# Sixteen normalised activation tiles are transposed by DMA instead of by TensorE and ScalarE, in a two-layer kernel on eight cores

## The chip, the cores and the metric

One Trainium2 chip, all 8 of its cores. Each core runs the same program on its own 2,048 of the 16,384 tokens; the weights are the same for all of them and each core loads all of them. The metric is the device time of the slowest core, in microseconds (us); smaller is better.

## The reference

```
x = x + layernorm(einsum('bsk,nk->bsn', layernorm(x), weight1 * elem_mask))
x = x + layernorm(einsum('bsi,oi->bso', layernorm(x), sign(weight2)) + bias)
# x: (2, 8192, 4096); weight1, weight2: (4096, 4096); elem_mask: 32 x 32 blocks of 0 or 1
```

Two layers, each a layer norm, a 4096 x 4096 matrix product, a second layer norm and a residual. The first product has a block mask on its weights, the second has the signs of its weights.

## The kernel before

A core's tokens are 16 tiles of 128. The output of a layer is made in 8 slabs of 512 columns, and a slab's weights are 8 blocks of 512 rows of the reduction. A **unit** is 8 tiles by one slab: 8 blocks x 8 tiles x 4 matmuls of 128x512, that is 256 matmuls, with the 8 PSUM banks holding the 8 tiles' sums. The units run in this order: 0 to 7 are slabs 0 to 3 of layer 1, for tiles 0 to 7 and 8 to 15 in turn; 8 to 11 are slabs 4 to 7 for tiles 0 to 7; 12 to 15 are slabs 4 to 7 for tiles 8 to 15; 16 to 23 are the eight slabs of layer 2 for tiles 0 to 7; 24 to 29 are six of them for tiles 8 to 15, and the last two slabs of those tiles are the tail.

So layer 1 is complete for tiles 0 to 7 when unit 12 begins, and for tiles 8 to 15 when unit 16 begins. The step between the layers is spread over the units: VectorE's `residual(tt)` scales the first product's row by its statistics, adds the loaded x and takes the statistics of the sum, for two tiles in each of units 12 to 15 and for one tile in each of units 16 to 23. GpSimd's queue loads the rows and stores the sum in DRAM (`store_x1`), ScalarE normalises it in place (`normalise`, L861), and after the unit's last matmul TensorE transposes it in 128x128 pieces (`transposes`, L464), eight to a PSUM bank, which ScalarE copies back into the tile's place in HT (`evict_transposed`, L837). Only the transposed form can be the stationary operand of layer 2.

ScalarE has two other jobs there. In layer 1 it evicts the sums of each unit (`evict1`, L847). In units 15 to 22 it turns the next unit's 16 weight **pieces** (128x1024 float32, 512 KB) into signs in fp8 (`sign_piece`, L853), in its program ahead of that unit's evictions. SyncE's queue loads the pieces (`load_w2`, L360) into **stages**, slots of 4 KB a partition: ST has stages 0 to 6, YS 7 and 8, RING 9 to 12. A piece's load waits until the work that had its stage last is done (`wait_stage_free`). The fixed table in `_homes` says which stage each piece gets: the first 16 pieces of layer 2, which are signed in unit 15, have stages 2, 3 and 4 in turn, and the others 5, 6, 2, 3 and 4. Before these loads, SyncE's queue holds the reloads of layer 1's last masked blocks (L417).

Every engine works through its own instructions in the order in which they are written, and semaphores order them between engines. `wait_acc_out` waits until a PSUM bank has been evicted. Signed blocks are kept in DRAM too, and the units from 24 on read them back (RING then has `NQ` slots of a signed block). ME holds layer 1's block mask, which nothing reads after its last weight piece.

Of the kernel before, what the change touches and what calls it, by code (L numbers as in the profile page):

```python
# [14 lines left out]
F32 = mybir.dt.float32  # L15
BF16 = mybir.dt.bfloat16
F8 = mybir.dt.float8e4
I32 = mybir.dt.int32
AF = mybir.ActivationFunctionType
AX = mybir.AxisListType  # L20

D = 4096
# [9 lines left out]


NRING = 10
NQ = 20
N2 = 96
U_A1 = 12
U_B1 = 16
# [28 lines left out]
for _u in range(2, 31):  # L67
    if _u in MASK_END:
        START[_u + 1] = (START[_u] + 2) % 8
    elif 16 <= _u < 24:  # L70
        START[_u + 1] = (START[_u] + 4) % 8
    else:
        START[_u + 1] = START[_u]

# [26 lines left out]

STAGES = 13
FEED_RING = (1, 4, 0, 2, 3, 5, 6)
HOME = {}
BEFORE = {}
# [2 lines left out]
def _homes():  # L110
    last, count = {}, {}

    def put(piece, at):
        sw = "p" if piece[0] == "x" else "s"
        count[sw, at] = count.get((sw, at), 0) + 1
        HOME[piece] = (at, count[sw, at])
        BEFORE[piece] = last.get(at)
        last[at] = piece

    for g in range(16):  # L120
        put(("m", g), ((0, 1, 5, 6), (9, 10, 11, 12))[g // 4 % 2][g % 4])
    for p in range(16):
        put(("w", p), (2, 3, 4, 7, 8)[p % 5])
    for g in range(16, 32):
        put(("m", g), (0, 1, 4)[(g - 16) % 3])
    last[2] = last[3] = ("xt", 13)
    last[5] = last[6] = ("xt", 14)
    k = 0
    for u in range(1, 11):
        for kind, n in FEED[u]:  # L130
            for piece in ([("m", n)] if kind == "m" else [("w", 2 * n), ("w", 2 * n + 1)]):
                put(piece, FEED_RING[k % 7])
                k += 1
    for g in range(32):
        put(("x", g), (0, 1, 5, 6)[g % 4])
    for g in range(32, 64):
        put(("x", g), g % 2)
    for p in range(16):
        put(("z", p), 2 + p % 3)
    for p in range(16, 128):  # L140
        put(("z", p), (5, 6, 2, 3, 4)[(p - 16) % 5])


_homes()
# [7 lines left out]

SEMS = (["cst", "msk_rd", "wgt", "sgn", "rdy_bt", "rdy_me", "msk_mm", "xaggr", "xstat", "xn0", "xn1",
         "tr", "tev", "mm", "blk", "ev1", "ev2", "bns", "self", "xp", "x1stat", "x1norm",
         "ystat", "yt", "fo", "pool"]
        + ["ldS%d" % i for i in range(STAGES)] + ["ldP%d" % i for i in range(STAGES)]
        + ["ldX%d" % i for i in range(16)] + ["ldR%d" % i for i in range(NRING)]
        + ["stC%d" % i for i in range(NRING)] + ["stY%d" % i for i in range(2)]
# [6 lines left out]
def build():  # L165
# [19 lines left out]
    with es:  # L185
# [28 lines left out]
        RING8 = RING[:, :].bitcast(F8)  # L214
        PBH = pb[:, :].bitcast(BF16)
        HTF = HT[:, :].bitcast(F32)
        YSF = YS[:, :].bitcast(F32)
        RINGF = RING[:, :].bitcast(F32)
        RINGI = RING[:, :].bitcast(I32)
# [20 lines left out]

        def stage(piece, ints=False):
            at = HOME[piece][0]
            if at >= 9:
                return RINGI[:, (at - 3) * 1024:(at - 2) * 1024]
            if at >= 7:
                return YSF[:, (at - 7) * 1024:(at - 6) * 1024]
            return (STI if ints else ST)[:, at * 1024:(at + 1) * 1024]
# [72 lines left out]
        def wait_stage_free(eng, piece):  # L320

            o = BEFORE[piece]
            if o is None:
                return
            kind, k = o
            if kind == "xt":
                eng.wait_ge(sem["xn1"], k + 1)
            elif kind == "m":
                eng.wait_ge(sem["msk_rd"], k + 1)
            elif kind == "w":  # L330
                eng.wait_ge(sem["wgt"], k + 1)
            elif kind == "x":
                eng.wait_ge(sem["xp"], k + 1)
            else:
                eng.wait_ge(sem["sgn"], k + 1)
# [112 lines left out]
        def _(t):  # L448
# [85 lines left out]
            for u in range(2, 30):  # L534
                lay, base, slab = unit(u)
                n0 = unit_block0(u)
                frees = u >= 8 or u % 2 == 1
                for b in range(8):
                    for p in range(8):
                        i = (START[u] + p) % 8  # L540
                        if b == 0:

                            if u == 2 and i >= 4:
                                if i == 7:
                                    t.wait_ge(sem["rdy_me"], 5)
                                else:
                                    t.wait_ge(sem["tev"], 64)
                            elif u == 2:
                                t.wait_ge(sem["ev1"], 8 + 4 + i + 1)
                            elif 13 <= u <= 16:  # L550
                                t.wait_ge(sem["tev"], 64 + 8 * (u - 13) + p + 1)
                            elif 17 <= u <= 24 and p >= 4:
                                t.wait_ge(sem["tev"], 96 + 4 * (u - 17) + p - 4 + 1)
                            else:
                                wait_acc_out(t, u - 1, i)
                            if u - 1 in MASK_END and p == 7:
                                t.wait_ge(sem["rdy_me"], masks)

                            if u == 16:
                                t.wait_ge(sem["tev"], 64 + 4 * i + 4)  # L560
                            if u == 24:
                                t.wait_ge(sem["tev"], 96 + 4 * i + 4)
                        if p == 0:
                            wait_block_ready(t, n0 + b)
                        ins = visit(i, base + i, n0 + b, b == 0, b == 7)
                        if b == 7:
                            ins.then_inc(sem["mm"], 1)
                        elif p == 7 and frees:
                            ins.then_inc(sem["blk"], 1)
                        if b == 7 and p == 3 and u in MASK_END:  # L570
                            s = MASK_END[u]
                            t.wait_ge(sem["msk_rd"], 16 * s + 16)
                            wait_acc_out(t, u, START[u])
                            mask_sums(START[u], s, range(4))
                if u in MASK_END:
                    masks += 1
                    t.wait_ge(sem["rdy_bt"], masks)
                    wait_acc_out(t, u, (START[u] + 1) % 8)
                    t.matmul(bank((START[u] + 1) % 8), SEL[:, :], BTD[:, :], start=True, stop=True
                             ).then_inc(sem["msk_mm"], 1)  # L580
                if 12 <= u < 16:
                    for q in range(8):
                        tt = 2 * (u - 12) + q // 4
                        if q % 4 == 0:
                            t.wait_ge(sem["x1norm"], tt + 1)
                        wait_acc_out(t, u, (START[u] + q) % 8)
                        transposes(tt, q % 4, (START[u] + q) % 8)
                if 16 <= u < 24:
                    t.wait_ge(sem["x1norm"], u - 8 + 1)
                    for q in range(4):  # L590
                        wait_acc_out(t, u, (START[u] + q) % 8)
                        transposes(u - 8, q, (START[u] + q) % 8)


            for i in range(8):
# [237 lines left out]
        def _(a):  # L833
# [21 lines left out]

            def normalise(tt):

                slot = HT[:, tt * D:(tt + 1) * D]
                a.wait_ge(sem["x1stat"], tt + 1)
                a.wait_ge(sem["stX%d" % (tt % 2)], 16 * (tt // 2 + 1))  # L860
                a.activation(slot, slot, AF.Identity, bias=NM[:, tt:tt + 1], scale=RS[:, tt:tt + 1]  # L861
                             ).then_inc(sem["x1norm"], 1)

            def scale_y(seq, h):

# [43 lines left out]

            for u in range(2, 30):  # L910
                lay, base, slab = unit(u)
                if 13 <= u <= 16:
                    for q in range(8):
                        evict_transposed(2 * (u - 13) + q // 4, q % 4, (START[u - 1] + q) % 8,
                                         64 + 8 * (u - 13) + q)
                if 17 <= u <= 24:
                    for q in range(4):
                        evict_transposed(u - 9, q, (START[u - 1] + q) % 8, 96 + 4 * (u - 17) + q)
                for b in range(8):
                    if 15 <= u < 23:  # L920
                        n = unit_block0(u + 1) + b
                        wait_ring_slot(a, n)
                        sign_piece(n, 0)
                        sign_piece(n, 1)
                    if 12 <= u < 16 and b in (3, 6):
                        normalise(2 * (u - 12) + (b == 6))
                    if 16 <= u < 24 and b == 6:
                        normalise(u - 8)
                for tt in FIN.get(u, ()):
                    scale_y(tt, 0)  # L930
                    scale_y(tt, 1)
# [214 lines left out]
```

## Time and profile before

| | |
|---|---|
| median of 3 runs (lowest to highest) | 1949.73 us (1949.58 to 1951.43) |
| time of the profiled execution, and its span | 1950.22 us, 1948.7 us |
| spans of the eight cores | 1937.1 to 1948.7 us |
| TensorE busy | 1859.5 us (95%) |
| matmuls of the two products | 8192, 1786.8 us busy |
| ScalarE busy | 484.5 us (25%) |
| VectorE busy | 967.1 us (50%) |
| DMA, mean over the span | 471.53 MB, 242 GB/s |

The profile is of the slowest core of one execution. Busy time is the time in which an engine has an instruction in work; the span runs from the first instruction to the last. The granted clock is a share of TensorE's full 2.4 GHz. DMA share is the mean busy share of the core's 16 DMA engines in a stretch. A row of the chain that ended last has a start in us, a length in us, and what was at work.

### The profile page before, as it was taken

How to read it: one execution, taken by the hardware profiler on the slowest of the kernel's cores; microseconds unless marked ns; L12 is line 12 of the kernel's file. 1: busy time of each engine (PE TensorE's matmuls, PEld its weight loads, DVE VectorE, ACT ScalarE, POOL GpSimd, SP SyncE). 2: the span in 40 equal slices, each digit the busy share in tenths (PEclk: the TensorE clock that was granted, in tenths of full speed). 3: DMA queues.
4: the chain of work that ended last, by engine and by line, in shares of the span. 5: the costliest groups of instructions: out<-in, count | busy, mean ns of one | idle time of the engine just before them, and what ended most of it. 6: DMA issues, size and time to landing. Idle time of an engine off the chain costs nothing.

```text
span 1948.7 us, 26135 instructions; the slowest of 8 cores (1937.1 to 1948.7 us)
## 1 busy us (share of the span) xinstructions
PE 1859.5 (95%) x9483; PEld 875.6 (45%) x9483; DVE 967.1 (50%) x1441; ACT 484.5 (25%) x449; POOL 230.6 (12%) x420
## 2 busy tenths in 40 slices
PE   2689999999999999999999999999999999999996
PEld 1245444444444444444445444444444444444442
DVE  5778477666564330665533534433552333342465
ACT  2266300000000000133445444434420011110032
POOL 2444100000011000110101000000001011000110
PEclk8899999999999999999999999999999999999998
DMA  9998689976698764787799988898863566562494
GB/s 295 330 311 295 182 284 323 302 220 237 228 313 261 248 200 141 236 257 229 234 274 285 294 275 288 278 314 279 266 213 114 194 227 207 187 200 71 141 284 164
DMA packets 121791, 471.53 MB, mean 242 GB/s; under 512 B 13600, under 2 KB 13616, under 8 KB 106304
## 3 DMA queue, kind: packets, MB, share of 16 engines
q1 hardware_dynamic: 85248, 289.44, 47.4%
q0 software_dynamic: 36416, 180.41, 26.9%
q8 instruction: 77, 1.26, 0.3%
q14 instruction: 50, 0.41, 0.1%
HBM read 354.46 MB, written 115.34 MB: 241 GB/s over the span
## 4 chain that ended last, share of the span: by engine, by line
PE 83%; DMA 9%; DVE 3%; SPq 2%; issue 1%; POOL 1%; ACT 1%; DVEq 0%; ACTq 0%; POOLq 0%
PE pb L474 81%; DMA ST<-w2s 2%; DMA RING<-x 2%; DMA ST<-w1s 2%; PE pb L464 2%; DMA HT<-x 1%; DVE BNX L670 1%; SPq L383 1%; SPq L349 1%; DVE RING L662 1%; DVE RR L638 1%; DMA ST<-mask 0%; DMA ST<-x 0%; PE pb L456 0%; POOL HT L974 0%
## 5 line engine op out<-in xcount | busy, mean ns | idle before, releaser
L474 PE MATMUL pb<-RING,HT 128*128 128x512 bf16 (+1 forms) x8192 | 1786.8, 380 | 21.7 <-DVE RING L662 18.0
L474 PEld LDWEIGHTS pb<-RING,HT 128*128 128x128 bf16 x8192 | 800.3, 98 | 985.9 <-issue 37.8
L760 DVE TENSOR_TENSOR YS<-pb,RR 128x512 bf16<-128x512 f32 x112 | 77.3, 691 | 335.0 <-PE pb L474 334.9
L686 DVE BATCH_NORM_STATS2 BNST<-YS 128x6 f32<-128x512 bf16 x240 | 150.2, 682 | 152.7 <-ACT YS L847 151.5
L847 ACT ACTIVATE YS<-pb 128x512 bf16<-128x512 f32 x128 | 74.7, 600 | 539.7 <-PE pb L474 539.4
L662 DVE TENSOR_TENSOR RING<-ST,ME 128x1024 bf16<-128x1024 f32 x122 | 145.0, 1222 | 102.8 <-PE pb L474 70.4
L853 ACT ACTIVATE RING<-ST 128x1024 fp8e4<-128x1024 f32 x128 | 132.1, 1067 | 179.4 <-DMA ST<-w2s 179.2
L876 ACT ACTIVATE ST<-HT,NM,RS 128x2048 f32<-128x2048 bf16 x32 | 65.7, 2088 | 382.1 <-DVE NM L630 378.7
L638 DVE TENSOR_REDUCE RR<-ST 128x32 f32<-128x1024 int32 x120 | 142.4, 1212 | 25.1 <-DMA ST<-mask 24.3
L837 ACT ACTIVATE HT<-pb 128x1024 bf16<-128x1024 bf16 x128 | 122.3, 1041 | 130.6 <-PE pb L464 130.5
L743 DVE TENSOR_TENSOR HT<-HT,ST 128x1024 bf16<-128x1024 bf16 x64 | 75.6, 1223 | 90.6 <-DMA ST<-x 87.5
L861 ACT ACTIVATE HT<-HT,NM,RS 128x4096 bf16<-128x4096 bf16 x16 | 60.8, 3798 | 150.5 <-DMA x1d<-HT 128.5
L770 DVE TENSOR_TENSOR ST<-ST,HT 128x2048 f32<-128x2048 f32 x32 | 72.3, 2290 | 41.7 <-ACT ST L876 41.6
L464 PE MATMUL pb<-IDN,HT 128*128 128x128 bf16 x1024 | 72.3, 231 | 20.6 <-POOL HT L974 7.1
L987 POOL DMA_DIRECT2D y1d<-YS x32 | 24.7, 771 | 502.0 <-ACT YS L847 502.0
L464 PEld LDWEIGHTS pb<-IDN,HT 128*128 128x128 bf16 x1024 | 66.7, 104 | 33.3 <-issue 25.3
L746 DVE BATCH_NORM_STATS2 BNX<-HT 128x6 f32<-128x512 bf16 x128 | 77.5, 681 | 1.7
L670 DVE BATCH_NORM_STATS2 BNX<-HT 128x6 f32<-128x512 f32 x96 | 58.5, 679 | 37.1 <-DMA HT<-x 23.1
L987 POOL DMA_DIRECT2D y2d<-YS x28 | 21.5, 769 | 434.7 <-DVE YS L760 431.9
L999 POOL DMA_DIRECT2D ST<-x x64 | 34.4, 538 | 156.0 <-DVE HT L743 153.9
L884 ACT ACTIVATE HT<-HT,NM,RS 128x2048 bf16<-128x2048 f32 x16 | 33.5, 2093 | 47.9 <-POOL NM L967 47.9
L1023 POOL DMA_DIRECT2D out<-ST x32 | 17.3, 540 | 185.3 <-DVE ST L770 185.3
(53 smaller groups left out, 335.1 us busy)
## 6 DMA issues: line engine op xcount, KB each, us to landing
ST<-w2s SPq DMA_DIRECT2D x128, 512.0 KB, 12.5
ST<-w1s SPq DMA_DIRECT2D x122, 512.0 KB, 10.5
ST<-mask SPq DMA_DIRECT2D x120, 512.0 KB, 9.7
ST<-x POOLq DMA_DIRECT2D x64, 512.0 KB, 11.1
out<-ST POOLq DMA_DIRECT2D x32, 1024.0 KB, 6.9
HT<-x SPq DMA_DIRECT2D x24, 1024.0 KB, 20.6
y1d<-YS POOLq DMA_DIRECT2D x32, 512.0 KB, 4.4
c1d<-RING POOLq DMA_DIRECT2D x32, 512.0 KB, 9.0
```

The source lines that it names most:

```text
L464: ins = t.transpose(PBH[:, b * 1024 + e * 128:b * 1024 + (e + 1) * 128], HT[:, c:c + 128], IDN[:, :])
L474: ins = t.matmul(bank(b), HT[:, c:c + 128], w[:, e * 512:(e + 1) * 512], start=(first and e == 0), stop=(last and e == 3))
L638: v.tensor_reduce(RR[:, (s % 2) * 512 + q * 32:(s % 2) * 512 + q * 32 + 32], stage(("m", g), True).rearrange("p (a b) -> p a b", b=32), AX ...
L662: v.tensor_tensor(dst, src, mk, op=OP.mult).then_inc(sem["wgt"], 1)
L670: ins = v.bn_stats(BNX[:, q * 6:q * 6 + 6], xhalf(k, q // 4)[:, (q % 4) * 512:(q % 4) * 512 + 512])
L686: v.bn_stats(BNST[:, c:c + 6], YS[:, i * 512:(i + 1) * 512]).then_inc(sem["bns"], 1)
L743: v.tensor_tensor(part, part, stage(piece), op=OP.add).then_inc(sem["xp"], 1)
L746: ins = v.bn_stats(BNX[:, q * 6:q * 6 + 6], slot[:, q * 512:(q + 1) * 512])
L760: v.tensor_tensor(YS[:, i * 512:(i + 1) * 512], bank(i), BIA[:, (slab % 2) * 512:(slab % 2) * 512 + 512], op=OP.add).then_inc(sem["ev2"], 1)
L837: a.activation(HT[:, c:c + 1024], PBH[:, b * 1024:(b + 1) * 1024], AF.Identity).then_inc(sem["tev"], 1)
L847: a.activation(YS[:, i * 512:(i + 1) * 512], bank(b), AF.Identity).then_inc(sem["ev1"], 1)
L853: a.activation(ring(n)[:, h * 1024:(h + 1) * 1024], stage(("z", p)), AF.Sign, saturate=False).then_inc(sem["sgn"], 1)
```

## The change

TensorE's transposes between the units 12 to 24 and ScalarE's copies of them back to HT are gone. `normalise(tt)` now writes its result to another room: to stages 2 and 3 of ST for tiles 0 to 7, and to the last two bf16 slots of RING for tiles 8 to 15. `transpose_back(tt)` then issues one transposing DMA of 128 x 4096 bf16 (1 MB) from ScalarE's queue, from the room into HT. The wait for the tile's store to DRAM has moved from `normalise` to it, and `normalise` waits until the DMA of the tile before has landed (`x1tr`), since the room is one. Unit 16 waits for the DMAs of tiles 0 to 7 and unit 24 for those of 8 to 15. The stages 2 and 3 aren't free in unit 15 any more: the first 16 pieces of layer 2 use stage 4 and a new stage 13, in ME, and the others six stages. RING has 16 slots for signed blocks in the place of 20.

```diff
-NQ = 20
+NQ = 16
@@ _homes
+    last[2] = last[3] = ("t", 7)
+    last[13] = ("w", 127)
...
     for p in range(16):
-        put(("z", p), 2 + p % 3)
+        put(("z", p), (4, 13)[p % 2])
     for p in range(16, 128):
-        put(("z", p), (5, 6, 2, 3, 4)[(p - 16) % 5])
+        put(("z", p), (5, 6, 2, 3, 4, 13)[(p - 16) % 6])
@@ wait_stage_free
-            if kind == "xt":
+            if kind == "t":
+                eng.wait_ge(sem["x1tr"], 16 * (k + 1))
+            elif kind == "xt":
@@ TensorE, block 0 of a unit
-                            elif 13 <= u <= 16:
-                                t.wait_ge(sem["tev"], 64 + 8 * (u - 13) + p + 1)
-                            elif 17 <= u <= 24 and p >= 4:
-                                t.wait_ge(sem["tev"], 96 + 4 * (u - 17) + p - 4 + 1)
                             else:
                                 wait_acc_out(t, u - 1, i)
...
-                            if u == 16:
-                                t.wait_ge(sem["tev"], 64 + 4 * i + 4)
-                            if u == 24:
-                                t.wait_ge(sem["tev"], 96 + 4 * i + 4)
+                            if u == 16 or u == 24:
+                                t.wait_ge(sem["x1tr"], 16 * (base + i + 1))
@@ TensorE, after a unit
-                if 12 <= u < 16:
-                    for q in range(8):
-                        tt = 2 * (u - 12) + q // 4
-                        if q % 4 == 0:
-                            t.wait_ge(sem["x1norm"], tt + 1)
-                        wait_acc_out(t, u, (START[u] + q) % 8)
-                        transposes(tt, q % 4, (START[u] + q) % 8)
-                if 16 <= u < 24:
-                    t.wait_ge(sem["x1norm"], u - 8 + 1)
-                    for q in range(4):
-                        wait_acc_out(t, u, (START[u] + q) % 8)
-                        transposes(u - 8, q, (START[u] + q) % 8)
@@ ScalarE
             def normalise(tt):
 
-                slot = HT[:, tt * D:(tt + 1) * D]
+                room = STB[:, 2 * 2048:4 * 2048] if tt < 8 else RING[:, 8 * 2048:10 * 2048]
                 a.wait_ge(sem["x1stat"], tt + 1)
+                if tt == 8:
+                    wait_block_free(a, 88)
+                    wait_block_free(a, 89)
+                if tt > 0:
+                    a.wait_ge(sem["x1tr"], 16 * tt)
+                a.activation(room, HT[:, tt * D:(tt + 1) * D], AF.Identity,
+                             bias=NM[:, tt:tt + 1], scale=RS[:, tt:tt + 1]).then_inc(sem["x1norm"], 1)
+
+            def transpose_back(tt):
+
+                room = STB[:, 2 * 2048:4 * 2048] if tt < 8 else RING[:, 8 * 2048:10 * 2048]
+                a.wait_ge(sem["x1norm"], tt + 1)
                 a.wait_ge(sem["stX%d" % (tt % 2)], 16 * (tt // 2 + 1))
-                a.activation(slot, slot, AF.Identity, bias=NM[:, tt:tt + 1], scale=RS[:, tt:tt + 1]
-                             ).then_inc(sem["x1norm"], 1)
+                a.dma_start_transpose(HT[:, tt * D:(tt + 1) * D].rearrange("p (k t) -> p k t", k=32),
+                                      room).then_inc(sem["x1tr"], 16)
@@ ScalarE, units 2 to 29
-                if 13 <= u <= 16:
-                    for q in range(8):
-                        evict_transposed(2 * (u - 13) + q // 4, q % 4, (START[u - 1] + q) % 8,
-                                         64 + 8 * (u - 13) + q)
-                if 17 <= u <= 24:
-                    for q in range(4):
-                        evict_transposed(u - 9, q, (START[u - 1] + q) % 8, 96 + 4 * (u - 17) + q)
                 for b in range(8):
...
                     if 12 <= u < 16 and b in (3, 6):
                         normalise(2 * (u - 12) + (b == 6))
-                    if 16 <= u < 24 and b == 6:
+                        transpose_back(2 * (u - 12) + (b == 6))
+                    if 16 <= u < 24 and b == 5:
                         normalise(u - 8)
+                    if 16 <= u < 24 and b == 7:
+                        transpose_back(u - 8)
```

`START`, the bank with which a unit begins, also stays the same from unit 16 to 24, where it moved on by 4 at each.

How the instructions stand. TensorE, from unit 7's last block to unit 13 before (L474 are the products' matmuls, L464 the transposes, L579 a product for the block mask):

```order
L474 MATMUL pb<-RING,HT 128x512 x16
L579 MATMUL pb<-BTD,SEL 128x512
L474 MATMUL pb<-RING,HT 128x512 x1280
L464 MATMUL pb<-IDN,HT 128x128 x64
L474 MATMUL pb<-RING,HT 128x512 x256
```

and now, from the same place to the end of the program:

```order
L480 MATMUL pb<-RING,HT 128x512 x16
L579 MATMUL pb<-BTD,SEL 128x512
L480 MATMUL pb<-RING,HT 128x512 x6144
L185 UNCONDITIONAL_BRANCH
```

The 512 transposes (4 times 64 and 8 times 32) have left TensorE, and the matmuls of units 8 to 29 and of the tail follow each other. ScalarE in unit 15 before, from the copies of unit 14's transposes to the middle of the unit (L853 signs a piece from the stage that it waits for, L861 normalises tile 6):

```order
L837 ACTIVATE HT<-pb 128x1024 [waits tr] x8
L853 ACTIVATE RING<-ST 128x1024 [waits blk,ldS2]
L853 ACTIVATE RING<-ST 128x1024 [waits ldS3]
L853 ACTIVATE RING<-ST 128x1024 [waits blk,ldS4]
L853 ACTIVATE RING<-ST 128x1024 [waits ldS2]
L853 ACTIVATE RING<-ST 128x1024 [waits mm,ldS3]
L853 ACTIVATE RING<-ST 128x1024 [waits ldS4]
L853 ACTIVATE RING<-ST 128x1024 [waits mm,ldS2]
L853 ACTIVATE RING<-ST 128x1024 [waits ldS3]
L861 ACTIVATE HT<-HT,NM,RS 128x4096 [waits x1stat,stX0]
```

and now, from unit 14's evictions to the middle of unit 15 (L841 signs a piece, L853 normalises tile 6, L861 issues its transposing DMA):

```order
L835 ACTIVATE YS<-pb 128x512 [waits mm,stY1,bns] x4
L841 ACTIVATE RING<-ST 128x1024 [waits blk,ldS4]
L841 ACTIVATE RING<-ME 128x1024 [waits ldS13]
L841 ACTIVATE RING<-ST 128x1024 [waits blk,ldS4]
L841 ACTIVATE RING<-ME 128x1024 [waits ldS13]
L841 ACTIVATE RING<-ST 128x1024 [waits mm,ldS4]
L841 ACTIVATE RING<-ME 128x1024 [waits ldS13]
L841 ACTIVATE RING<-ST 128x1024 [waits mm,ldS4]
L841 ACTIVATE RING<-ME 128x1024 [waits ldS13]
L853 ACTIVATE ST<-HT,NM,RS 128x4096 [waits x1stat,x1tr]
L861 DMA_TRANSPOSE HT<-ST 128x32x128 [waits x1norm,stX0]
```

The eight copies ahead of the signs have gone, the pieces now alternate between two stages where there were three, and the DMA stands right behind the normalising, ahead of the next pieces. ScalarE in unit 12 now:

```order
L853 ACTIVATE ST<-HT,NM,RS 128x4096 [waits x1stat]
L861 DMA_TRANSPOSE HT<-ST 128x32x128 [waits x1norm,stX0]
L853 ACTIVATE ST<-HT,NM,RS 128x4096 [waits x1stat,x1tr]
L861 DMA_TRANSPOSE HT<-ST 128x32x128 [waits x1norm,stX1]
L835 ACTIVATE YS<-pb 128x512 [waits mm,stY0,bns] x4
```

Tile 1's normalising waits for tile 0's DMA, and the unit's evictions stand behind both DMA issues.

## Rows read from the trace of the kernel before

**Rows 1.** The page: engines busy, with share and instructions

```profile
PE 1859.5 (95%) x9483; PEld 875.6 (45%) x9483; DVE 967.1 (50%) x1441; ACT 484.5 (25%) x449; POOL 230.6 (12%) x420
```

**Rows 2.** The chain that ended last, 844 to 1558 us

```profile
844.52 3.57 PE pb L464 x64
848.09 55.25 PE pb L474 x256
903.34 3.57 PE pb L464 x64
...
1086.71 1.79 PE pb L464 x32
1088.49 55.25 PE pb L474 x256
...
1485.98 1.79 PE pb L464 x32
```

**Rows 3.** TensorE in order of time, end of unit 15 (start, us, what)

```profile
965.58 55.42 PE L474 MATMUL pb<-RING,HT 128*128 128x512 bf16 x256
1024.97 6.49 PE L464 MATMUL pb<-IDN,HT 128*128 128x128 bf16 x64 [3.97 <-ACT YS L847]
1031.29 55.42 PE L474 MATMUL pb<-RING,HT 128*128 128x512 fp8e4 x256
```

**Rows 4.** The same chain within unit 15

```profile
971.31 7.75 DMA ST<-w2s
...
980.27 10.98 DMA ST<-w2s
...
992.47 10.66 DMA ST<-w2s
...
1004.34 9.36 DMA ST<-w2s
...
1014.90 7.29 DMA ST<-w2s
```

**Rows 5.** ScalarE in order of time, from unit 14's evictions to unit 15's

```profile
962.38 0.60 ACT L847 ACTIVATE YS<-pb 128x512 bf16<-128x512 f32 x1 [0.27 <-PE pb L474]
962.87 7.43 ACT L837 ACTIVATE HT<-pb 128x1024 bf16<-128x1024 bf16 x8
970.10 3.02 ACT L853 ACTIVATE RING<-ST 128x1024 fp8e4<-128x1024 f32 x3
979.14 1.06 ACT L853 ACTIVATE RING<-ST 128x1024 fp8e4<-128x1024 f32 x1 [6.02 <-DMA ST<-w2s]
...
1018.67 3.79 ACT L861 ACTIVATE HT<-HT,NM,RS 128x4096 bf16<-128x4096 bf16 x1
1022.36 1.99 ACT L853 ACTIVATE RING<-ST 128x1024 fp8e4<-128x1024 f32 x2
1024.25 3.99 ACT L847 ACTIVATE YS<-pb 128x512 bf16<-128x512 f32 x8
```

**Rows 6.** Line L360 (loads of pieces), 945 to 1025 us: ns min/median/max

```profile
L360 SPq DMA_DIRECT2D ST<-w2s x20: 327/328/734, 948.9 to 1024.9; - x20
DMA to landing us min/median/max: 6.6/8.9/16.0
```

**Rows 7.** ScalarE in order of time, unit 12

```profile
822.61 3.80 ACT L861 ACTIVATE HT<-HT,NM,RS 128x4096 bf16<-128x4096 bf16 x1 [32.54 <-DMA x1d<-HT]
838.69 3.80 ACT L861 ACTIVATE HT<-HT,NM,RS 128x4096 bf16<-128x4096 bf16 x1 [12.28 <-DMA x1d<-HT]
842.40 3.99 ACT L847 ACTIVATE YS<-pb 128x512 bf16<-128x512 f32 x8
```

**Rows 8.** One stretch, seven periods of units 16 to 22, all engines

```profile
1031.00:1430.00 399.00, 399.00 (x2015) 187.57 (x2012) 165.84 (x305) 168.60 (x149) 33.06 (x56) 1.00 0.90 286
```

**Rows 9.** DMA queue of the hardware-issued loads; then a 1 MB store's landing (us)

```profile
q1 hardware_dynamic: 85248, 289.44, 47.4%
...
x1d<-HT POOLq DMA_DIRECT2D x16, 1024.0 KB, 10.5
```

**Rows 10.** TensorE in order of time, from unit 24 to the end

```profile
1487.61 442.19 PE L474 MATMUL pb<-RING,HT 128*128 128x512 fp8e4 x2048
```

More of the change, by code:

```diff
@@ L69 @@
         START[_u + 1] = (START[_u] + 2) % 8
-    elif 16 <= _u < 24:
-        START[_u + 1] = (START[_u] + 4) % 8
     else:
@@ L98 @@
 FEED = _feed()
-STAGES = 13
+STAGES = 14
 FEED_RING = (1, 4, 0, 2, 3, 5, 6)
@@ L154 @@
          "tr", "tev", "mm", "blk", "ev1", "ev2", "bns", "self", "xp", "x1stat", "x1norm",
-         "ystat", "yt", "fo", "pool"]
+         "ystat", "yt", "fo", "pool", "x1tr"]
         + ["ldS%d" % i for i in range(STAGES)] + ["ldP%d" % i for i in range(STAGES)]
@@ L216, in build @@
         HTF = HT[:, :].bitcast(F32)
+        MEF = ME[:, :].bitcast(F32)
+        STB = ST[:, :].bitcast(BF16)
         YSF = YS[:, :].bitcast(F32)
@@ L242, in stage @@
             at = HOME[piece][0]
+            if at == 13:
+                return MEF[:, 0:1024]
             if at >= 9:
```

## The prediction, made before the changed kernel ran

> **What bounds the kernel now.** I read the profile's page first: TensorE is busy for 1859.5 of 1948.7 us, and no other engine for more than half of the span [rows 1]. So the time is what stands in TensorE's queue, and what makes it wait. The chain that ended last shows that queue around the change: from unit 12 on it alternates between 256 matmuls of 55.25 us and a batch of transposes, 3.57 us for 64 (twice in a row in the chain, and a third time after unit 14) and 1.79 us for 32, eight times from 1086.71 to 1485.98 us [rows 2]. So a transpose costs 55.8 ns there, and nothing stands between. The timeline of TensorE shows one exception [rows 3]: unit 15's matmuls end at 965.58 + 55.25 = 1020.83 us, TensorE waits for ScalarE's first eviction until 1024.97, then needs 6.49 us for the 64 transposes instead of 3.57 (granted clock below full after the pause), and unit 16 starts near 1031.4, 10.6 us after unit 15's end. The chain in unit 15 says why: it runs through five waits for loads of w2 pieces [rows 4], because ScalarE signs 16 pieces through three stages ahead of its evictions [rows 5]. After unit 24 TensorE has 2048 matmuls without a gap [rows 10], and the change touches nothing there but the number of ring slots.
>
> **What the change can save.** Three batches of 3.57 us, the 10.6 us around unit 15's end, and eight of 1.79 us: 10.7 + 10.6 + 14.3 = 35.6 us at most. ScalarE's copies leave too, but it has time to spare except in unit 15.
>
> **Units 12 to 14: -10.7 us, if the DMA is in time.** The DMA's waits come ahead of the evictions. In unit 12 tile 0's store had landed at 822.61 us and tile 1's at 838.69, since the normalising that waited for them starts there [rows 7]. Now tile 0's DMA is issued at 822.6, tile 1's normalising needs it landed, and tile 1's DMA is issued at 838.7; then the evictions can start. TensorE needs the first at about 844.5. So there are 838.7 - 3.8 - 822.6 = 12.3 us for the first DMA to land, and 5.2 us for the issue of the second to hold ScalarE's queue. The trace has no transposing DMA, so I bound both from rows. Landing: the nearest row is the 1 MB store, 10.5 us at its median [rows 9]; that is in time. Holding of the queue: below, an issue on SyncE's queue, 0.33 us [rows 6]; above, the 10.5 us to the landing. I take 5, the middle: no stall in unit 12, and none in 13 and 14, where more time lies between. At the upper end unit 12 pays 5.3 us and the same clock loss as in [rows 3], 2.9 us.
>
> **Unit 15: 7 to 8 us of its period kept, 3 of it lost again.** This is where the change also takes something away. Before, signing began at 970.10 us behind the eight copies; unit 14's evictions had ended at 962.98 [rows 5]. Without two batches ahead of it (7.1 us) that end is now 955.9. The first two pieces are there; from then each pair of pieces must be loaded into the two stages after the pair before it has been signed. With three stages a load in the chain took 7.75 to 10.98 us, mean 9.2 [rows 4]. With two loads out, not three, it is shorter: not below 6.1 (two thirds of 9.2, if nothing is fixed), and the fastest there was 6.6 [rows 6]. I take 7.0. A round is then 7.0 + 1.06 + 0.1 = 8.2 us, seven rounds are 57.4, and with the first piece and the last two (1 + 2.1) signing would end at 1016.4. Two normalisings with DMA issues stand between: each holds ScalarE for 3.8 + 5 us, of which the loads in flight cover 7.0, so 1.8 twice: 1020.0. Unit 15's matmuls now end at 1020.8 - 10.7 = 1010.1, so TensorE waits until 0.75 us after the signs, which is how long it took before from ScalarE's first eviction at 1024.25 to TensorE's start at 1024.97 [rows 3, 5]: 1020.8. It loses 2.9 us more by its clock, as it did after the shorter pause of [rows 3]. Unit 16 starts as if at 1023.7, where it was at 1031.4: **7.7 us are gained by then, so the 10.7 of the units before are kept but for 3.0.** The bounds: with 6.1 us a load and 0.3 us a hold, TensorE hardly waits, and the gain by unit 16 is about 20; with 9.2 us and 10.5 us, signing ends at 955.9 + 1 + 7 x 10.4 + 2.1 + 2 x 5.1 = 1042.0, unit 16 starts at 1045.7, and 14.3 us are lost by then.
>
> **Units 16 to 23: -14.3 us, if the DMA engines can carry it.** ScalarE now has 16 signs, a normalising and an issue in a unit of 55.25 us: 17 + 3.8 + 5, enough room. VectorE evicts here, as before. The DMA engines are the question. From 1031 to 1430 us they are busy for 0.90 of the time at 286 GB/s [rows 8], which is 51.3 us in a period of 57.04. A transposing DMA adds 1.05 MB. At the rate of these rows (286 / 0.90 = 318 GB/s) it is 3.3 us, and 51.3 + 3.3 = 54.6 fits into 55.25. Up to 57.04 - 51.3 = 5.7 us a unit may be used before these units are slower than they were. The upper bound: the destination of the DMA is in runs of 128 bf16, 256 bytes, so 4096 of them a tile, 256 for each of 16 engines; if each took what a packet of queue q1 takes now, 0.474 x 16 x 1948.7 us / 85248 = 173 ns [rows 9], a tile would occupy all engines for 44 us. I take the lower value for the forecast, as a move of the same bytes is the nearest row, and keep the other as a rival.
>
> The row on this is the 0.90 at 286 GB/s [rows 8]; the Trainium skill has two figures for the transposing DMA itself, which no row here shows. "DMA: Bandwidth & Descriptors" (Latency and other measured facts) has 261 GB/s, measured in one kernel; by that a tile is 4.0 us, an estimate, and a unit 55.3: the same sum. The skill's "VectorE: DVE Perf Modes" (The three transpose paths) speaks against the change: it has 1309 ns for one 128x128 block by DMA; 32 of them one behind another are 41.9 us a tile, an estimate, and the sum is that of the slow rival below.
>
> **Ring slots and stages after unit 16: 0.** Each unit's eight blocks still fit beside the next one's (8 + 8 = 16). SyncE's queue in unit 16 stops at piece 18 until tile 7's DMA has landed, and the piece's block is needed a whole unit later. In the tail the last slab's blocks wait for unit 29's, and are needed from 6.9 us after its end on, one each 0.86 us.
>
> **Sum.** -7.7 - 14.3 = -22.0 us. The profiled execution took 1950.22 us, so 1928.2; it stood 0.5 us above the median of the runs, so 1927.7 there. I say 1928.
>
> **Rivals.**
> - *The DMA is cheap but held up* (0.14). It lands 20 us or so after its issue, behind other traffic, or its issue holds ScalarE until it lands. Then unit 12 pays some 8 us, unit 15's bound applies (14.3 lost in place of 7.7 gained), and 14.3 comes back: 1950.2 + 8 + 14.3 - 14.3 = 1958, between 1940 and 1975 as the landing goes from 12 to 20 us. For it speaks that a 1 MB store takes 10.5 us to land where its bytes need 3.3 [rows 9]; against it that units 13 and 14 have much more time.
> - *The transposing DMA is slow* (0.24): small runs, each with a fixed cost. It decides from 5.7 us of all engines, or 12.3 us to land. At 44 us a tile, unit 12 ends 822.6 + 44 + 3.8 + 0.6 - 844.5 = 26.5 us late, units 13 to 15 take 2 x 47.8 instead of 55.25 us (where their period was 58.8: +37 each), and seven units of layer 2 take 51.3 + 44 instead of 57.04 (+38 each): 1950 + 23 + 110 + 268, about 2350 us. At 10 us a tile only the latter counts: +4.3 x 7 and unit 15's bound, about 1990. No row excludes it; for it speaks only the bound by packets.
> - *Everything in time* (0.10): unit 15 signs in 51 us, and 34 of the 35.6 us come out: 1916.
> - *The forecast* (0.52), with its own range 1917 to 1940.
>
> **Range and chances.** 1915 to 2010 us: it leaves out most of the slow rival and a little below. Faster by over 0.2% (3.9 us, about what a measurement of this kernel can tell from no change): 0.52 + 0.10 = 0.62. Within 0.2%: 0.05, from the held-up case. Slower: 0.33, which is the slow rival and the rest of the held-up one.
>
> **What would show it.** In the profile after: no gap at the ends of units 12, 13, 14 and of 16 to 22, matmul batches 55.25 us apart; a gap of about 11 us before unit 16, released by ScalarE's eviction behind signs that wait for w2 loads; x1tr seldom waited for; landing of the transposing DMA near 10 us; DMA share near 0.98 in units 16 to 22. I am wrong if ScalarE's evictions wait behind a DMA issue or behind x1tr, if a transposing DMA needs more than some 6 us of the engines, or if unit 15's loads don't get shorter with two out.

## The result, and the profile after

The changed kernel is slower: 1.0876 times the time before, 95% interval 1.0792 to 1.096 (about 2121 us by that ratio). Times and ratios here leave out the executions in which the cores of one die got a lower granted clock than the others, as in two of the changed kernel's seven (2252.74 and 2305.39 us). The other five took 2107.49 to 2133.17 us, a wider spread than the 2 us of the kernel before. The forecast was 1928 us in a range to 2010: wrong in sign and outside the range. What happened is the slow rival, at less than half of the loss that I gave it (171 us, where it had 400). The profiled execution took 2133.17 us, its slowest core's span is 2131.6 us.

The page of the changed kernel, to be read beside [rows 1] and the first row of [rows 9]: busy time of the engines, then the DMA queues, of which q10 is new and carries the transposing DMAs alone.

```profile
PE 1854.9 (87%) x8971; PEld 849.5 (40%) x8971; DVE 964.0 (45%) x1441; ACT 421.8 (20%) x385; POOL 230.1 (11%) x420
...
q1 hardware_dynamic: 85248, 289.44, 44.7%
q0 software_dynamic: 36416, 180.41, 24.4%
q10 hardware_dynamic: 66048, 16.78, 12.1%
```

TensorE has 512 matmul instructions less and is busy for a smaller share. The 16 DMAs are 66048 packets, 4128 each, of 1.05 MB: 256 bytes a packet, where q1 moves 3.4 KB in one. For 16.78 MB the time of these packets is 12.1% of the 16 engines' span, 0.121 x 2131.6 / 16 = 16.1 us a tile. That is an upper value of what the engines lose by it: packets can overlap, and the DMA share from 1160 to 1620 us is 1.06, more than the whole.

TensorE in order of time, to be read beside [rows 2, 3]:

```profile
779.72 71.17 PE L480 MATMUL pb<-RING,HT 128*128 128x512 bf16 x329
888.43 58.13 PE L480 MATMUL pb<-RING,HT 128*128 128x512 bf16 x256 [37.53 <-ACT YS L835]
985.18 57.54 PE L480 MATMUL pb<-RING,HT 128*128 128x512 bf16 x256 [38.62 <-ACT YS L835]
1077.28 57.57 PE L480 MATMUL pb<-RING,HT 128*128 128x512 bf16 x256 [34.56 <-ACT YS L835]
1156.30 112.57 PE L480 MATMUL pb<-RING,HT 128*128 128x512 fp8e4 x512 [21.45 <-ACT YS L835]
1270.09 55.41 PE L480 MATMUL pb<-RING,HT 128*128 128x512 fp8e4 x256 [1.22 <-DVE YS L748]
1342.14 44.44 PE L480 MATMUL pb<-RING,HT 128*128 128x512 fp8e4 x192 [16.64 <-ACT RING L841]
```

Where 3.57 us of transposes stood after the units 12, 13 and 14, TensorE now waits 37.5, 38.6 and 34.6 us for an eviction by ScalarE, and 21.5 after unit 15. Later it waits for signed weights. The waits of TensorE from 780 to 1700 us, summed by what ended them (us, times, longest):

```profile
PE pb L480 <- ACT YS L835: 132.2, 4, 38.6
PE pb L480 <- ACT RING L841: 49.0, 6, 16.6
PE pb L480 <- DMA HT<-RING: 7.4, 1, 7.4
PE pb L480 <- DVE YS L748: 1.2, 1, 1.2
```

That is 189.8 us, and 2 to 3 us more at each of the long waits of the units 12 to 14, since the unit after it runs partly below the full granted clock (58.13, 57.54 and 57.57 us instead of 55.4). Against it stand the 35.6 us of batches and gaps that left. ScalarE in order of time shows why it is late, beside [rows 7] (ACTq is ScalarE's queue while it issues a DMA):

```profile
822.89 3.80 ACT L853 ACTIVATE ST<-HT,NM,RS 128x4096 bf16<-128x4096 bf16 x1 [26.45 <-DVE NM L618]
829.33 28.69 ACTq L861 DMA_TRANSPOSE HT<-ST  x1
878.53 3.80 ACT L853 ACTIVATE ST<-HT,NM,RS 128x4096 bf16<-128x4096 bf16 x1 [51.83 <-DMA HT<-ST]
882.46 4.91 ACTq L861 DMA_TRANSPOSE HT<-ST  x1
887.58 4.03 ACT L835 ACTIVATE YS<-pb 128x512 bf16<-128x512 f32 x8 [5.25 <-issue]
```

Tile 0's DMA is issued at 829.3 and has landed 49 us later; tile 1's normalising waits for it, and unit 12's evictions behind that. The issue itself holds the queue for 28.7 us. But tile 1's DMA, the same instruction, is issued in 4.9 us. The DMA view of the two stretches, 829 to 878 and 979 to 986 us (tile 3's DMA), tells them apart (GB/s is in 40 slices; issues end with us to landing):

```profile
GB/s 428 207 300 157 181 45 43 86 100 88 103 143 129 108 148 222 255 227 271 301 311 304 267 253 279 283 242 177 153 132 80 68 72 40 42 35 38 177 25 33
...
ST<-x POOLq DMA_DIRECT2D x4, 512.0 KB, 33.6
RING<-c1d SPq DMA_DIRECT2D x4, 512.0 KB, 29.6
x1d<-HT POOLq DMA_DIRECT2D x1, 1024.0 KB, 39.7
```

```profile
GB/s 0 0 0 0 0 0 0 0 69 224 224 215 212 203 222 215 215 214 221 222 218 217 212 217 219 217 228 215 214 212 218 222 227 214 209 195 84 0 0 0
DMA packets 4128, 1.05 MB, mean 150 GB/s; under 512 B 4128, under 2 KB 4128, under 8 KB 4128
...
HT<-ST ACTq DMA_TRANSPOSE x1, 6.7
```

Alone, a tile lands in 6.7 us, at some 217 GB/s. Beside other traffic the first DMA of each pair in the units 12 to 14 takes 49.1, 60.9 and 55.7 us, and the others slow down with it: 8.0 MB in 49 us are 164 GB/s, where the kernel before moved 269 GB/s from 820 to 870 us, and a 1 MB store lands in 39.7 us instead of 10.5 [rows 9]. The stall is what lets the second DMA of a pair run alone: GpSimd's and SyncE's queues have run dry behind the waiting tile by then.

### The profile page after: what moved, and what is told of

The parts are those of the page before. It is cut to its first block, busy times and chain, and to the rows that moved or that the text cites. A ratio compares the mean times of both kernels' runs of the same rounds, so it can differ in the third digit from the quotient of the medians.

```text
span 2131.6 us, 24952 instructions; the slowest of 8 cores (2066.2 to 2131.6 us)
## 1 busy us (share of the span) xinstructions
PE 1854.9 (87%) x8971; PEld 849.5 (40%) x8971; DVE 964.0 (45%) x1441; ACT 421.8 (20%) x385; POOL 230.1 (11%) x420
## 3 DMA queue, kind: packets, MB, share of 16 engines
q10 hardware_dynamic: 66048, 16.78, 12.1%
## 4 chain that ended last, share of the span: by engine, by line
PE 46%; DMA 28%; ACTq 12%; DVE 4%; ACT 3%; issue 2%; another core or an unknown queue 2%; SPq 2%; POOL 1%; DVEq 0%; POOLq 0%
PE pb L480 45%; ACTq L861 12%; DMA ST<-w2s 9%; DMA ME<-w2s 4%; DMA ST<-x 3%; DMA HT<-ST 2%; DMA HT<-RING 2%; DMA ST<-w1s 2%; DMA x1d<-HT 2%; ACT RING L841 1%; DMA HT<-x 1%; DVE BNX L658 1%; DMA HT<-y1d 1%; ACT ST L853 1%
## 5 line engine op out<-in xcount | busy, mean ns | idle before, releaser
L480 PE MATMUL pb<-RING,HT 128*128 128x512 bf16 (+1 forms) x8192 | 1811.4, 384 | 212.2 <-ACT YS L835 134.8
L841 ACT ACTIVATE RING<-ST 128x1024 fp8e4<-128x1024 f32 x102 | 104.7, 1054 | 336.3 <-issue 174.3
L853 ACT ACTIVATE ST<-HT,NM,RS 128x4096 bf16<-128x4096 bf16 x8 | 30.4, 3796 | 233.5 <-DMA HT<-ST 170.8
L825 ACT ACTIVATE HT<-pb 128x1024 bf16<-128x1024 bf16 x64 | 62.2, 1023 | 43.1 <-PE pb L470 43.1
L983 POOL DMA_DIRECT2D y2d<-YS x28 | 21.5, 768 | 438.9 <-DVE YS L748 436.1
L470 PE MATMUL pb<-IDN,HT 128*128 128x128 bf16 x512 | 38.9, 232 | 17.3 <-POOL HT L970 9.1
L470 PEld LDWEIGHTS pb<-IDN,HT 128*128 128x128 bf16 x512 | 34.1, 105 | 27.1 <-issue 21.6
L853 ACT ACTIVATE RING<-HT,NM,RS 128x4096 bf16<-128x4096 bf16 x8 | 30.3, 3789 | 49.1 <-DMA HT<-RING 25.9
## 6 DMA issues: line engine op xcount, KB each, us to landing
ST<-x POOLq DMA_DIRECT2D x64, 512.0 KB, 12.1
```

The source lines that it names most:

```text
L480: ins = t.matmul(bank(b), HT[:, c:c + 128], w[:, e * 512:(e + 1) * 512], start=(first and e == 0), stop=(last and e == 3))
L841: a.activation(ring(n)[:, h * 1024:(h + 1) * 1024], stage(("z", p)), AF.Sign, saturate=False).then_inc(sem["sgn"], 1)
L853: a.activation(room, HT[:, tt * D:(tt + 1) * D], AF.Identity, bias=NM[:, tt:tt + 1], scale=RS[:, tt:tt + 1]).then_inc(sem["x1norm"], 1)
```

## The experiments

The theory that I set out from: the transposing DMA goes in 256-byte packets, each of which waits its turn behind a packet of another queue, and the 16 engines keep step. Its rivals: the added volume as such; the two stages and 16 ring slots; small pieces, with no need for step.

**One DMA beside chosen traffic.** Behind the last store of the kernel before, one DMA at a time:

```diff
+                a.dma_start_transpose(HT[:, 13 * D:14 * D].rearrange("p (k t) -> p k t", k=32),
+                                      HT[:, 12 * D:13 * D]).then_inc(sem[name], 16)
...
+                s.dma_start(HTF[:, j * 1024:(j + 1) * 1024], w2_d[j // 2, :, (j % 2) * 1024:(j % 2) * 1024 + 1024]
+                            ).then_inc(sem[name], 16)
```

> The kernel before, with seven stretches added behind its last store, in which ScalarE's queue issues one 1 MB DMA from one slot of HT to another while nothing else runs but what is named. (0) transposing, alone; (1) transposing beside 24 loads of 512 KB on SyncE's queue in rows of 4 KB; (2) the same beside loads of the same bytes in rows of 1 KB; (3) transposing beside 24 such loads of 4 KB rows on GpSimd's queue; (4) transposing beside 10 loads into one partition each, 23 rows of 4 KB, which a single DMA engine carries; (5) a plain copy alone; (6) a plain copy beside the loads of (1). Theory 1, turns: the transposing DMA goes in 256-byte packets, 256 on each of 16 engines, each of which waits for one packet of the other queue, and the engines keep step; so about 6.7 us in (0), 256 x 0.17 = 43 us or until the other loads end in (1) and (3), about a third of it in (2) if rows are packets, and 30 to 40 us in (4) with all engines slow together (some 30 to 40 GB/s throughout). Theory 2, volume: 1 MB is 1 MB; (1), (2), (3) and (6) all land in about 10 us, (4) near 7. Without step between the engines (4) shows 200 GB/s for 5 us and a long thin rest.

Landings on the slowest core: (0) alone 6.8 us; (1) beside 4 KB rows on SyncE's queue 48.0; (2) beside 1 KB rows 15.6; (3) beside GpSimd's queue 15.6; (4) beside one busy engine 39.8; (5) plain copy alone 4.7; (6) plain copy beside the loads of (1) 8.6. The answers on (1), with the two queues in its middle, 1963 to 1999 us:

```profile
L977 ACTq DMA_TRANSPOSE HT<-HT x1: 35122/35122/35122, 1955.6 to 1955.6; - x1
DMA to landing us min/median/max: 48.0/48.0/48.0
...
q1 hardware_dynamic: 2904, 10.59, 93.8%
q10 hardware_dynamic: 2902, 0.74, 9.1%
```

The DMA view of (4), first 2100 to 2143 us, then the queues from 2106 to 2132 us:

```profile
GB/s 0 121 151 42 35 50 50 48 47 49 50 49 49 47 52 49 46 53 49 46 49 49 50 48 51 50 45 50 54 45 50 47 26 24 28 25 24 27 27 0
...
DMA packets 2707, 1.28 MB, mean 49 GB/s; under 512 B 2554, under 2 KB 2554, under 8 KB 2707
...
q10 hardware_dynamic: 2547, 0.65, 145.0%
q1 hardware_dynamic: 160, 0.63, 5.9%
```

Volume is out: 48.0 against 8.6 us for the same bytes beside the same loads. The packets of the others matter: a quarter of their size, a third of the landing. (1) shows the turns: in those 36 us 2902 small packets went beside 2904 of the loads, one for one. It shows also that turns alone don't slow the others: all traffic moved at 278 GB/s over its 49 us, against 303 over 45 us beside the plain copy (6). And (4) shows the step. The loads keep one engine at work (5.9% of 16 engines is 0.94 of one) and move 160 packets in 26 us; the transposing DMA moves 2547 in that time, 159 for each of 16 engines. So each engine waits for the one that takes turns with the loads, and the 49 GB/s are half loads, half transposing: 0.65 MB in 26 us are 25 GB/s, where it ran at 217 alone. Had the other 15 gone on by themselves, a burst of 5 us and a thin rest would stand there. A small packet's time includes this waiting: alone it is 0.797 x 7 x 16 / 4128 = 0.022 us, here 1.45 x 26 x 16 / 2547 = 0.24 us.

I had expected 43 us for (3) too, and it was 15.6. GpSimd's first load was issued 0.85 us behind the DMA, but the view of 2053 to 2058.5 us has no packet of its queue yet:

```profile
q10 hardware_dynamic: 3161, 0.81, 83.6%
```

So 3161 of the DMA's 4128 packets had started before there was anything to take turns with. (3) says little of GpSimd's queue.

The Trainium skill, "DMA: Bandwidth & Descriptors" (Queues, rings and completion order), says that each DMA engine goes round the queues that have work and drains a packet from one before it turns to the next. If the profile's packets are taken for its packets, (1), (2) and (4) agree; in (2), from 2010 to 2018 us, it is 1913 packets beside 1912. Its "Advanced Engine Details and Errata" (X-Bar Transpose (TRN2)) has "TRN2 transpose DMAs are as fast as regular DMAs". The measurements differ: alone 6.8 against 4.7 us, beside a full queue 48.0 against 8.6.

**The same copy without the transposing.**

```diff
-                a.dma_start_transpose(HT[:, tt * D:(tt + 1) * D].rearrange("p (k t) -> p k t", k=32),
-                                      room).then_inc(sem["x1tr"], 16)
+                a.dma_start(HT[:, tt * D:(tt + 1) * D], room).then_inc(sem["x1tr"], 16)
```

> The changed kernel with a plain 1 MB copy from the room to HT in the place of each transposing DMA (layer 2 then works on rows that are not transposed); all waits, stages and bytes stay. Theory 1 (turns of small packets): the copies land in about 10 us, the units of layer 1 have no gap, and the kernel comes to what I had predicted, 1920 to 1935 us. Theory 2 (volume): the DMA engines carry the same bytes, so it stays above 2050 us. Theory 3 (two stages and 16 ring slots are what costs): it also stays well above 1950.

Measured 0.9914 times before (0.9893 to 0.9935), about 1934 us: faster. TensorE in order of time, then one stretch that answers to [rows 8], then q10:

```profile
851.92 165.92 PE L480 MATMUL pb<-RING,HT 128*128 128x512 bf16 x752 [1.83 <-ACT YS L835]
1025.49 9.04 PE L480 MATMUL pb<-RING,HT 128*128 128x512 fp8e4 x28 [7.65 <-ACT YS L835]
1036.71 663.63 PE L480 MATMUL pb<-RING,HT 128*128 128x512 fp8e4 x3074 [2.18 <-DMA HT<-ST]
```

```profile
1020.00:1400.00 380.00, 372.33 (x1712) 168.09 (x1713) 165.71 (x307) 147.39 (x127) 33.83 (x57) 0.99 0.98 319
```

```profile
q10 hardware_dynamic: 2304, 16.78, 2.1%
```

The plan of the change stands with a DMA that costs what its bytes cost: the batches between the units are gone, unit 15 has a gap of 7.7 us, and the DMA engines carry the added megabytes at a share of 0.98 and 319 GB/s. A tile's packets take 0.021 x 1933.7 / 16 = 2.5 us of them. So the whole loss, from 0.99 to 1.09, lies in the transposing DMA.

**The same pieces without the transposing.** Two plain DMAs of 256-byte pieces a tile, in another order:

```diff
+                for h in range(2):
+                    a.dma_start(HT[:, tt * D:(tt + 1) * D].rearrange("p (b a t) -> p b a t", a=2, t=128)[:, :, h, :],
+                                room[:, h * 2048:(h + 1) * 2048].rearrange("p (b t) -> p b t", t=128)
```

> The changed kernel with two plain DMAs in the place of each transposing one, which move the same 1 MB in pieces of 256 bytes, in another order, and so not transposed. If small pieces are enough (theory 1, turns): landing of 30 to 60 us beside other traffic, and 2050 us or more, like the changed kernel. If it needs the crossing of the transposing path, or if the queue joins such pieces into larger packets: 1920 to 1960 us, as the plain copy.

Measured 1.0053 (1.0037 to 1.0069), between the two answers and near the second. Its q10 has as many packets as the changed kernel's, and its landings are spread nearly as widely (6.7 to 62.7 us there, 30.1 at the median), but the time of its packets is a third:

```profile
q10 hardware_dynamic: 66048, 16.78, 4.0%
...
DMA to landing us min/median/max: 4.2/18.3/54.5
```

0.040 x 1961.7 / 16 = 4.9 us a tile against 16.1. Small packets make the DMA late (+1.4% on the plain copy), and their issue can be held too, for up to 20.4 us. They don't make the others late: from 780 to 1430 us a 512 KB load of x landed after 10.3 us at the median, where it was 11.5 before. Another 8% come with the transposing alone, which fits engines that keep step; how much of it is the longer hold of ScalarE's queue and how much the slowed loads, no run separates. The theory needed both halves, and I had expected the first to weigh more.

**The stages alone.** TensorE transposes as before; the table of stages and `NQ = 16` are the changed kernel's.

```diff
-        put(("z", p), 2 + p % 3)
+        put(("z", p), (4, 13)[p % 2])
```

> The kernel before with the changed one's table of stages (4 and 13 for the first 16 pieces, six for the others) and 16 ring slots, and the transposes on TensorE as before. Theory 1: only unit 15 gets longer, by the two stages. My sizing (7.0 us a load, a round of 8.2) gives an end of signing near 1028 us against 1024 before, so +4 us, 1953; with loads of 9.2 us +20, 1970. Theory 3 (the stages are what costs): above 2050.

Measured 1.0051 (1.0033 to 1.0069), +10 us, where my sizing said +4: two stages cost something, and are no cause of the loss. TensorE's batch before unit 16 then starts after 9.5 us of waiting, where it was 3.97 in [rows 3].

**Half of the change, and the other half.** A list of tiles decides who transposes each, 0 to 7 in the one kernel and 8 to 15 in the other:

```diff
+TURNED = (0, 1, 2, 3, 4, 5, 6, 7)
...
-                if 12 <= u < 16:
+                if 12 <= u < 16 and 2 * (u - 12) not in TURNED:
```

> Half of the change: only tiles 0 to 7 (units 12 to 15) are transposed by DMA, from stages 2 and 3, with the changed table of stages; tiles 8 to 15 stay with TensorE, and the ring keeps 20 slots. Theory (turns in step, landing of 50 to 60 us beside other traffic): the loss is mostly here, since ScalarE's evictions stand behind the second normalising, which waits for the first DMA: gaps of 35 to 40 us after units 12, 13 and 14 and 20 after 15, in all +100 to +130 us. Rival (the DMA engines' time in units 16 to 22 is what costs): under +30 us.

Measured 1.0687 (1.065 to 1.0724), +134 us, a little above the range. TensorE waits 44.9, 51.8, 34.8 and 20.8 us at the ends of the units 12 to 15, and the units after 16 run as before.

> The other half: only tiles 8 to 15 (units 16 to 23) are transposed by DMA, from ring slots 8 and 9, with 16 ring slots; tiles 0 to 7 stay with TensorE, and the stages are those of before. Theory: a DMA in step takes 16 us of all engines, where only 5.7 are free in a unit, so 10 us more in each of seven units less what overlaps: +30 to +70 us. Rival (nothing but the evictions behind the DMA costs): no more than +10, or a gain of up to 14 us.

Measured 1.0206 (1.016 to 1.0252), +40 us. The two excesses, 6.87% and 2.06%, add to 8.9%, the whole is 8.8%. In the first half the cost is the evictions behind the landing; in the second signed weights are late, behind slowed loads and ScalarE's held queue: TensorE waits 8.2, 2.8, 11.4 and 12.6 us for them, and 31.5 us at last for a tile (the profiled execution took 2016.17 us, more than the 1984.82 and 2002.12 us behind the ratio, so only the order of size counts). The landing is shorter there, 30.3 us at the median, and a whole unit lies between landing and need, which covers most of it.

**A fourth stage and nothing else.**

```diff
-        put(("z", p), 2 + p % 3)
+        put(("z", p), (2, 3, 4, 13)[p % 4])
```

> No transposing DMA: the kernel before, with the new stage 13 as a fourth stage for the first 16 pieces (2, 3, 4, 13) and a sixth for the others. If the wait before unit 16 is set by the number of stages, as going from three to two (+10 us) says, a fourth takes most of the 10.6 us between the units away except the transposes' 3.57 to 6.5: -4 to -7 us, 1943 to 1946. If it is set by the DMA engines' share (0.93), nothing changes.

Measured 0.9987 (0.9978 to 0.9997). The wait before unit 16 is gone in the profile, on all cores; but the kernel gains 2.5 us, not 4 to 7. The slowest core of this execution lost 4.3 us at the end of unit 12 instead, and the row of [rows 3] was that of the slowest core alone: before, four of the eight didn't wait there at all. It is still the fastest of the versions here that transpose every tile.

**A quiet DMA.** Tiles 0 to 5 only, issued on SyncE's queue between block loads; GpSimd's queue waits from the tile's store to the landing.

```diff
+                if n in (77, 80, 85, 88, 93, 95):
+                    transpose_back(s, (77, 80, 85, 88, 93, 95).index(n))
...
+                if tt in TURNED:
+                    g.wait_ge(sem["x1tr"], by_dma(tt))
```

> Tiles 0 to 5 alone are transposed by DMA, and other traffic is kept away from it: it is issued on SyncE's queue between two block loads, so that these stand in line with it, and GpSimd's queue issues nothing between the store of a tile and the landing of its DMA. Four stages (4, 13, 2, 3) for the first pieces; tiles 6 to 15 stay with TensorE. Theory (it is slow only beside another queue's packets): each DMA lands in 7 to 15 us, no gap after units 12 to 14, -10.7 us, and with the stages' -5 in all 1930 to 1940. Rival (the transposing DMA is slow whenever TensorE and the loads work, whatever the queue): landing of 30 us or more, and slower than before by 50 us or more.

Measured 1.004 (1.0024 to 1.0056). TensorE, then all six DMAs:

```profile
779.63 235.85 PE L507 MATMUL pb<-RING,HT 128*128 128x512 bf16 x1092
1036.28 5.08 PE L497 MATMUL pb<-IDN,HT 128*128 128x128 bf16 x64 [20.79 <-ACT YS L881]
```

```profile
HT<-ST SPq DMA_TRANSPOSE x6, 6.8
```

The mechanism came out as expected: 6.8 us at the median and 8.4 at most, in the units in which the first DMA of each pair took 49 to 61, with TensorE and VectorE at work, and no gap until the end of unit 15. The forecast of the time failed all the same: the DMA of tile 5 stands in SyncE's queue until 966.1 us, so the first load for unit 16 is issued at 971.8 us instead of 948.9, and TensorE pays 20.8 us there.

**The same for four tiles.**

> As the quiet version, but for tiles 0 to 3 alone (units 12 and 13), so that no transposing DMA stands in SyncE's queue ahead of the first w2 loads, and with the stages 2, 3, 4 and 13 for the first pieces. Theory: landing under 10 us, no gap after units 12 and 13, nothing lost in unit 15; against the kernel with four stages alone two batches of 3.57 us less: some 7 us faster, 1940 to 1945. Rival (holding GpSimd's and SyncE's queues costs as much as the transposes): level with it or slower.

Measured 1.0027 (1.0016 to 1.0038). The DMAs land in 6.7 to 8.6 us, but the rival is right: GpSimd's queue waits 93.2 us in all for the four landings, so the stores of tiles 4 and 5 are late, and on the slowest core unit 14 ends with 12.5 us of waiting for an eviction behind them. Against the kernel with four stages alone (0.9987) it is some 8 us slower, though two batches, 7.1 us, are saved: the quiet costs about twice what the transposes did.

**In line with SyncE's loads, GpSimd's queue not held.**

> The quiet version of six tiles without the hold on GpSimd's queue: the DMA still stands in line with SyncE's loads, but GpSimd's loads and stores of 4 KB packets run beside it. Theory (turns with another queue's packets): landing goes back to 20 to 60 us, SyncE's queue is held as long, and the block loads of layer 1 come late: slower than the quiet version by 20 us or more. Rival (it was the distance from ScalarE's queue that helped): as the quiet version.

Measured 1.0114 (1.009 to 1.0138), some 14 us slower than the quiet version where I had said 20 or more.

```profile
817.38 38.58 SPq L296 DMA_TRANSPOSE HT<-ST  x1
877.97 4.91 SPq L296 DMA_TRANSPOSE HT<-ST  x1
908.45 17.62 SPq L296 DMA_TRANSPOSE HT<-ST  x1
```

One landing takes 56.6 us again, and TensorE waits 37.1 us behind it; the others take 9.2 to 21.8 us. So it is GpSimd's packets that make the DMA late, on SyncE's queue too, though here only one landing is as late as on ScalarE's.

## Why the prediction was wrong, step by step

- **What bounds the kernel, and what can be saved.** Right as a reading: the plain copy takes the batches away and is faster, by 17 us where the sum said 22. Its gap at unit 15 is 7.7 us where I had 10.7, and 2.2 us more go to a wait for a tile's landing, which I had at nothing.
- **The step that failed** is the price of the transposing DMA: "I take the lower value for the forecast, as a move of the same bytes is the nearest row". Bytes were the wrong likeness. Its packets take up to 16.1 us of all engines a tile, not 3.3; the first of each pair lands after 49 to 61 us in units 12 to 14, not 10.5; and it holds ScalarE's queue for 28.7 to 49.4 us there, not 5. Behind all three stand the 256-byte packets that take turns with the others': the plain DMAs in 256-byte pieces have late landings and held issues from the turns alone, and the rest comes with the step. That a DMA alone holds the queue for 4.8 to 5.0 us, as I had it, is luck: my 5 was the middle of two other rows.
- **The upper bound** of 44 us was near to the landing, from the right row and for another reason. I took 173 ns as a small packet's own cost; alone it costs 6.7 us / 256 = 26 ns. The rest is the wait for the large packet whose turn it is, 26 us / 160 = 163 ns in (4).
- **Units 12 to 14.** The chain of waits was right, and so was its margin of 12.3 us to land. The margin was missed by 37 us, and TensorE's gap is that: 37.5.
- **Unit 15.** Right in size: a round of two loads took 8.5 us with the plain copy (963.3 to 1022.6 us in seven rounds), where I had 8.2. (The loads in [rows 4] go from 7.29 us, not 7.75; their mean of 9.2 stands.) The stages alone cost 10 us, of which my rounds gave 4.
- **Units 16 to 23.** The limit of 5.7 us a unit was the right test: 2.5 us a tile passes it, at a share of 0.98 as forecast, and the transposing DMA does not. But its 16.1 us overstate the loss: by the limit seven units would lose 73 us, and the half with tiles 8 to 15 lost 40, or 54 with the 14.3 that were to be saved.
- **The slow rival** had the mechanism that decides, small runs, and a price of 2350 us that was too high by some 230. In units 12 to 15 I let every DMA cost 44 us, but the stall empties the other queues, and the second of each pair ran alone in 6.7. In seven units of layer 2 I let it cost 38 us each, 268 in all, as if nothing else moved meanwhile; the half with tiles 8 to 15 has some 54. The held-up rival had the held issue and the wait behind other traffic, but let the landing go to 20 us only. I gave the slow one 0.24 and said that no row excluded it; the range should have held more of it.

## What to carry to other kernels

Price a DMA by its packets and by what shares the engines with it, not by its bytes: ask how long the runs are (here 128 bf16, 256 bytes), and multiply their number on an engine by the time of one packet of the busiest other queue (here 256 x 0.163 = 42 us, an estimate, for (4)'s 39.8). A transposing DMA was cheap here only where the other queues were empty; a unit between its landing and its need did not save it, since it slows the loads meanwhile. In this kernel 32 transposes on TensorE cost 1.79 us a tile in the open, and neither a crowded DMA nor a quiet one beat that. And put the issue of a DMA that may be held where nothing urgent stands behind it in that queue.

## What was not expected of the hardware

- One busy DMA engine slows a transposing DMA on all 16: 25 GB/s instead of 217, with 15 engines otherwise idle.
- The harm can go both ways: beside tile 0's DMA a 512 KB load of x landed after 33.6 us at the median, where it was 9.3 from 820 to 870 us before, and the sum of all traffic fell to 164 GB/s. Beside loads that keep all 16 engines alike at work, as in (1), the sum stayed at 278 GB/s.
- The issue of a transposing DMA is not free of its progress: 4.8 to 5.0 us alone, up to 49.4 us beside others (62.8 in the half with tiles 0 to 7), while a plain copy's was 0.47 us. A plain DMA in 256-byte pieces is between: 0.6 to 20.4 us.
